# A decoder layer on one core: first and last rows of every engine's queue written as sequences of their own, weights prepared step by step between them

## The reference

```python
# attention: 8 heads of 128; x is (32, 112, 256), wq, wk, wv (256, 8, 128), wo (8, 128, 256)
q, k, v = einsum(layernorm(x), wq), einsum(.., wk), einsum(.., wv)
q, k = rope(rmsnorm(q)), rope(rmsnorm(k))
p = softmax(q k^T / 128 with a causal mask)
x = x + (p v) wo
# the context (32, 375, 256) serves as both weights of a two-layer net
h = layernorm(x) @ ctx^T
x = x + gelu_tanh(h) @ ctx
# a quantised feed-forward net (FFN): 256 -> 1024 -> 256
xq = fixed_quant(layernorm(x), 8, 4); w1q, w2q, b1q, b2q = fixed_quant(.., 8, 6)
x = x + fixed_quant(relu(fixed_quant(xq @ w1q^T + b1q)), 8, 4) @ w2q^T + b2q
```

## Time and profile before

| | |
|---|---|
| median of 3 runs | 654.29 us (653.25 to 656.85) |
| the profiled execution | 654.7 us, its span 652.9 us |
| PE, matmuls | 593.3 us busy, 91% |
| DVE | 588.1 us busy, 90% |
| ACT | 543.0 us busy, 83% |
| POOL | 348.0 us busy, 53% |
| mean granted PE clock | 0.974 |

### The profile page before, as it was taken

How to read it: one execution, slowest core, us unless ns; L and a number is a source line. 1 busy time by engine, 2 the same in 40 slices (tenths; PEclk the granted TensorE clock), 3 DMA queues, 4 the chain that set the end, 5 groups by cost and what they waited for, 6 DMA issues and landing times.

```text
span 652.9 us, 13103 instructions
## 1 busy us (share of the span) xinstructions
PE 593.3 (91%) x4624; PEld 477.3 (73%) x4624; DVE 588.1 (90%) x1339; ACT 543.0 (83%) x1402; POOL 348.0 (53%) x430
## 2 busy tenths in 40 slices
PE   1746889999999999999999999999999999997864
PEld 1424667777887788888778877888887788776753
DVE  3768899999999999999999999999999999998442
ACT  6675788999999999989998899999889999998522
POOL 1134555665555565666655555656666555556111
PEclk9967999999999999999999999999999999999978
DMA  8071566766776766667687676666677777666451
GB/s 296 0 200 36 114 139 138 137 138 150 149 148 137 147 133 142 141 141 153 133 151 152 143 152 138 137 142 132 143 149 138 150 152 146 134 141 138 89 109 37
DMA packets 222641, 88.92 MB, mean 136 GB/s; under 512 B 200704, under 2 KB 217552, under 8 KB 222320
## 3 DMA queue, kind: packets, MB, share of 16 engines
q1 hardware_dynamic: 222576, 88.08, 63.6%
HBM read 34.84 MB, written 3.67 MB: 59 GB/s over the span
## 4 chain that ended last, share of the span: by engine, by line
DVE 75%; ACT 9%; PE 5%; POOL 3%; issue 3%; DMA 3%; SPq 0%; ACTq 0%; DVEq 0%
DVE turn_s L433 11%; DVE turn_c L425 8%; DVE qk L524 8%; DVE o L550 5%; DVE ss L566 5%; DVE turn_c L614 5%; DVE ss L603 5%; DVE qk L639 4%; DVE h_t L590 2%; DVE y_out L545 2%; DVE g L628 2%; DVE x L634 2%; DVE stat L534 1%; POOL turn_c L354 1%; DVE xn L600 1%
## 5 line engine op out<-in xcount | busy, mean ns | idle before, releaser
L912 PE MATMUL psum<-wqkv,xT 128*112 128x512 f16 x384 | 148.3, 386 | 12.5 <-DMA xT<-xn 9.1
L913 PE MATMUL psum<-wqkv,xT 128*112 128x512 f16 x384 | 147.4, 384 | 0.0
L914 PE MATMUL psum<-wqkv,xT 128*112 128x512 f16 x384 | 147.1, 383 | 0.0
L354 POOL TENSOR_TENSOR turn_c<-turn_c,turn_s 112x1024 f32<-112x1024 f32 x32 | 75.7, 2365 | 48.4 <-DVE turn_s L433 48.4
L912 PEld LDWEIGHTS psum<-wqkv,xT 128*112 128x112 f16 x384 | 50.7, 132 | 43.4 <-DMA xT<-xn 9.7
L425 DVE TENSOR_TENSOR turn_c<-psum,cos_t 112x1024 f32<-112x1024 f32 x64 | 77.8, 1215 | 0.0
L433 DVE TENSOR_TENSOR turn_s<-psum,sin_t 112x1024 f32<-112x1024 f32 x64 | 77.7, 1214 | 0.0
L914 PEld LDWEIGHTS psum<-wqkv,xT 128*112 128x112 f16 x384 | 50.7, 132 | 34.1 <-issue 1.9
L922 PE MATMUL psum<-wo,oT 128*112 128x256 f16 x256 | 71.0, 277 | 4.7 <-DMA oT<-o 3.5
L524 DVE SCALAR_TENSOR_TENSOR qk<-turn_c,rms,qk 112x128 f16<-112x128 f32 x256 | 69.2, 343 | 2.6 <-ACT qk L796 2.5
L924 PE MATMUL psum<-wo,oT 128*112 128x256 f16 x256 | 71.0, 277 | 0.0
(11 more groups left out here) (107 smaller groups left out, 1699.2 us busy)
## 6 DMA issues: line engine op xcount, KB each, us to landing
ctxT<-in_ctx_cols SPq DMA_DIRECT2D x32, 375.0 KB, 3.4
ctx_in<-in_ctx_rows SPq DMA_DIRECT2D x32, 375.0 KB
x_in<-in_x SPq DMA_DIRECT2D x32, 112.0 KB, 2.3
out_y<-y_out SPq DMA_DIRECT2D x32, 112.0 KB, 2.9
w_raw<-in_w SPq DMA_DIRECT2D x2, 1024.0 KB, 6.1
w_raw<-in_wk SPq DMA_DIRECT2D x2, 512.0 KB, 5.0
...
```

What stands on the lines that cost most here:

```text
L354: pool.tensor_tensor(turn_c[:, 1, :], turn_c[:, 1, :], turn_s[:, 1, :], ALU.add).then_inc(k_turned, 1)
L912: pe.matmul(dst, hi, wqkv[:, 0, c, w, cols], start=c == 0, stop=False)
L913: pe.matmul(dst, hi, wqkv[:, 1, c, w, cols], start=False, stop=False)
L914: last = pe.matmul(dst, lo, wqkv[:, 0, c, w, cols], start=False, stop=c == MC - 1)
```

## The change

The three loops over bodies become, on each of the five engines, start(), the loop `for i in range(5, B - 5): body(i)` with the full bodies in the old order and without the `inside` tests, and end(). start() and end() list the calls of the first and last rows one by one, in an order of their own for each engine. The weight steps are cut into smaller calls and stand in start() among the batches' steps; each weight has semaphores of its own. w2 is now staged in w_raw where wq was and w1 where wk was, each loaded as soon as that weight is split; the weights' sums go to PSUM bank 6 (v0's) instead of 2. Where the new order no longer implies what a step needs, a wait is added for those batches, and others are dropped. No arithmetic is added or left out. The diff, cut to its core:

```diff
-        place = w_raw[:, :, :, :].rearrange("p c w n -> p (c w n)")
-        w1_raw = place[:, 0:2 * HD]
-        w2_raw = place[:, 2 * HD:4 * HD]
+        w1_raw = w_raw[:, :, 1, :]
+        w2_raw = w_raw[:, :, 0, :]
...
-        w_sum_ps = psum[:, 2, 0:4]
+        w_sum_ps = psum[:, 6, 0:4]
...
+            def load_w1():
+                sp.wait_ge(w_lo_done[1], MC)
+                sp.dma_start(w1_raw, w1_cols.rearrange("p (c n) -> p c n", c=MC)).then_inc(w1_in, 16)
+
+            def load_w2():
+                sp.wait_ge(w_lo_done[0], MC)
+                sp.dma_start(w2_raw, w2_cols.rearrange("p (c n) -> p c n", c=MC)).then_inc(w2_in, 16)
...
             def load_ctxT(j):
+                if j.off == 2:
+                    sp.wait_ge(h_ready, done(j.plus(-2)))
...
             def transpose_xq(j):
                 sp.wait_ge(xq_done, done(j))
+                if j.off == B - 4:
+                    sp.wait_ge(f1_ready, done(j.plus(-1)))
+                if j.off == B - 1:
+                    sp.wait_ge(f0_ready, done(j.plus(-1)))
...
             def load_ctx(j):
+                if j.off >= B - 4:
+                    sp.wait_ge(ctxout_ready, done(j.plus(-2)))
...
                 sp.wait_ge(xn_lo_done, done(j))
                 if j.has(1):
                     sp.wait_ge(v1_ready, done(j.plus(-1)))
+                if 2 <= j.off <= 4 or j.off == B - 1:
+                    sp.wait_ge(v0_ready, done(j.plus(-1)))
                 sp.dma_start_transpose(xT16[:, :, :], xn16[:, :, :].rearrange("t l n -> t (l n)")).then_inc(xT_landed, 16)
...
+            def start():
+                load_projection(1, 0)
+                load_projection(0, 1)
+                load_projection(1, 1)
+                load_projection(0, 0)
+                load_x(Batch(0))
+                load_projection(2, 0)
+                load_projection(2, 1)
+                load_x(Batch(1))
+                load_x(Batch(2))
+                load_tables()
+                load_ctxT(Batch(0))
+                load_ident()
+                transpose_x(Batch(0))
+                load_x(Batch(3))
+                load_wo()
+                load_ctxT(Batch(1))
+                load_w2()
+                transpose_x(Batch(1))
+                transpose_q(Batch(0))
+                transpose_k(Batch(0))
+                transpose_x(Batch(2))
+                transpose_q(Batch(1))
+                transpose_k(Batch(1))
+                transpose_o(Batch(0))
+                load_ctx(Batch(0))
+                load_biases()
+                transpose_x(Batch(3))
+                load_x(Batch(4))
+                transpose_k(Batch(2))
+                transpose_q(Batch(2))
+                transpose_o(Batch(1))
+                load_ctxT(Batch(2))
+                transpose_x(Batch(4))
...
+                transpose_k(Batch(B - 1))
+                transpose_q(Batch(B - 1))
+                store_out(Batch(B - 7))
+                transpose_o(Batch(B - 2))
+                load_ctxT(Batch(B - 2))
+                load_ctx(Batch(B - 2))
+                transpose_xq(Batch(B - 4))
+                load_ctxT(Batch(B - 1))
+                store_out(Batch(B - 6))
+                transpose_o(Batch(B - 1))
+                load_ctx(Batch(B - 1))
+                store_out(Batch(B - 5))
+                transpose_xq(Batch(B - 3))
+                store_out(Batch(B - 4))
+                transpose_xq(Batch(B - 2))
+                transpose_xq(Batch(B - 1))
+                store_out(Batch(B - 3))
+                store_out(Batch(B - 2))
+                store_out(Batch(B - 1))
+
+            start()
...
@@ vector
+            def start():
+                bound_weights(1)
+                stats_x(Batch(0))
+                lift_weights(1)
+                normalise_x(Batch(0))
+                stats_x(Batch(1))
+                bound_weights(0)
+                split_xn(Batch(0))
+                split_projection(1, 0)
+                lift_weights(0)
+                split_projection(1, 1)
+                normalise_x(Batch(1))
+                stats_x(Batch(2))
+                bound_weights(2)
+                split_projection(0, 0)
+                lift_weights(2)
+                split_xn(Batch(1))
+                split_projection(0, 1)
+                split_projection(2, 0)
+                sum_squares_k(Batch(0))
+                turn_sin_k(Batch(0))
+                turn_cos_k(Batch(0))
+                split_projection(2, 1)
+                bound_weights(3)
+                sum_squares_q(Batch(0))
+                turn_cos_q(Batch(0))
+                turn_sin_q(Batch(0))
+                turn_q(Batch(0))
+                normalise_x(Batch(2))
+                stats_x(Batch(3))
+                split_q(Batch(0))
+                split_k(Batch(0))
+                sum_squares_k(Batch(1))
+                turn_cos_k(Batch(1))
+                turn_sin_k(Batch(1))
+                sum_squares_q(Batch(1))
+                turn_sin_q(Batch(1))
+                split_xn(Batch(2))
+                turn_cos_q(Batch(1))
+                turn_q(Batch(1))
+                normalise_x(Batch(3))
+                split_q(Batch(1))
+                lift_weights(3)
+                invert_sums(Batch(0))
+                split_k(Batch(1))
+                turn_sin_k(Batch(2))
+                sum_squares_k(Batch(2))
+                split_o(Batch(0))
+                turn_cos_k(Batch(2))
+                unit_of_y()
+                split_wo()
+                turn_sin_q(Batch(2))
+                sum_squares_q(Batch(2))
+                turn_cos_q(Batch(2))
+                split_xn(Batch(3))
...
+                split_k(Batch(B - 1))
+                split_q(Batch(B - 1))
+                residual_attention(Batch(B - 3))
+                stats_x2(Batch(B - 3))
+                clip_hidden1(Batch(B - 6))
+                gelu_inner(Batch(B - 4))
+                split_o(Batch(B - 2))
+                gelu_outer(Batch(B - 4))
+                residual_out(Batch(B - 6))
+                normalise_x2(Batch(B - 3))
+                residual_ctx(Batch(B - 4))
+                stats_x3(Batch(B - 4))
+                clip_hidden0(Batch(B - 5))
+                gelu_inner(Batch(B - 3))
+                quantise_x3(Batch(B - 4))
+                clip_x3(Batch(B - 4))
+                invert_sums(Batch(B - 1))
+                residual_attention(Batch(B - 2))
+                split_o(Batch(B - 1))
+                gelu_outer(Batch(B - 3))
+                clip_hidden1(Batch(B - 5))
+                stats_x2(Batch(B - 2))
+                residual_out(Batch(B - 5))
+                normalise_x2(Batch(B - 2))
+                residual_ctx(Batch(B - 3))
+                stats_x3(Batch(B - 3))
...
@@ scalar
+            def start():
+                square_projection(1, 0)
+                square_projection(1, 1)
+                square_projection(0, 0)
+                square_projection(0, 1)
+                round_projection(1, 0)
+                round_xn(Batch(0))
+                square_projection(2, 0)
+                round_projection(1, 1)
+                square_projection(2, 1)
+                round_projection(0, 0)
+                round_projection(0, 1)
+                round_xn(Batch(1))
+                round_projection(2, 0)
+                square_k(Batch(0))
+                round_projection(2, 1)
+                square_wo(0)
+                square_wo(1)
+                square_q(Batch(0))
+                scale_k1(Batch(0))
+                scale_k0(Batch(0))
+                copy_v0(Batch(0))
+                copy_v1(Batch(0))
+                round_q1(Batch(0))
+                round_q0(Batch(0))
+                round_xn(Batch(2))
+                round_k0(Batch(0))
+                square_k(Batch(1))
+                round_weights(1)
+                square_q(Batch(1))
+                scale_k0(Batch(1))
+                scale_k1(Batch(1))
+                softmax_exp(Batch(0))
+                round_q1(Batch(1))
+                round_q0(Batch(1))
+                round_k0(Batch(1))
+                square_k(Batch(2))
+                normalise_o1(Batch(0))
+                normalise_o0(Batch(0))
+                round_o(Batch(0))
+                copy_v1(Batch(1))
...
+                softmax_exp(Batch(B - 1))
+                relu0(Batch(B - 5))
+                square_h(Batch(B - 3))
+                normalise_o1(Batch(B - 1))
+                normalise_o0(Batch(B - 1))
+                round_o(Batch(B - 1))
+                relu1(Batch(B - 5))
+                tanh_h(Batch(B - 3))
+                relu1(Batch(B - 4))
+                copy_xn2T(Batch(B - 2))
...
@@ tensor
             def project_k(j):
                 pe.wait_ge(xT_landed, landed_once(j))
-                if j.has(3):
+                if 3 <= j.off <= 5 or j.off >= 7:
                     pe.wait_ge(x2_done, done(j.plus(-3)))
+                if j.off == 0:
```

(88 more changed lines are left out.)

1155 lines of the change are left out of this document (847 added, 308 removed).

## The result

Timed in turn with the kernel before on the same chip, 20 runs each, the changed kernel took 656.90 us (653.48 to 659.67) against 654.79 (653.25 to 657.75): a ratio of 1.0033 [1.0017, 1.0048], so 2.2 us slower where 13 us faster were forecast, and outside the range of 627 to 652. Single runs of one kernel lie up to 6 us apart, the longer ones at a lower granted clock (of the changed kernel, the 11 runs at a mean clock of 0.975 to 0.978 have a median of 658.0, the 7 at 0.982 to 0.988 one of 656.1), so what follows rests on ratios and on the order of events inside a profile, not on one profile's total. The profiled run of the changed kernel is one of 657.78.

What follows compares the result with a forecast made beforehand. Bodies were taken as full on PE and VectorE, leaving at most 61 us of idle time at the ends; 654.7 - 6.0 (start) - 7.0 (end) = 641.7, less 0.4 for the median: 641.3 us, range 627 to 652.

Steps and rivals of the forecast that it cites:

- I take -6.0 for hitches that a walk misses: Start: the walk put its end 7 or more us earlier; -6.0 was taken to allow for hitches.
- The walk up to k(2): Start: new queues followed with old durations; first matmuls of k(0), k(1), k(2) at 17.65, 35.4, 50.2 us.
- the wait for exp_done(0): Start: a new wait said to set batch 2's first k projection at 50.2 us, 10.9 earlier.
- From here DVE is full: Start, k(3) to k(5): VectorE full and carrying put-off work; projections at 71.0, 87.0 and 106.0 us, the last -7.8.
- The walk's mark for VectorE: Start: split_q(3) ends at 91.2 us instead of 99.55; VectorE's gain is -6.0 net of put-off work.
- the mark k(2): Start: first matmul of batch 2's k projection, forecast at 50.2 us instead of 61.06.
- rival D: Whole kernel: no gain, as the first bodies give back what was won before; 654 us, chance 0.06.
- Rival A: Start: gaps of 2.1 to 3.8 us drop PE's clock in batches 0 to 3; 663 us, chance 0.08.
- The GELU of 28 releases ctx_out(28) at 602.7 [...] and scores(31) now stands before ctx_hidden(29): 604.3: End, PE: batch 31's scores start at 604.3 us, 3.1 earlier than before.
- The forecast's 36.1: End: invert_sums(31) at 609.8 us and the span's end at 645.9, 36.1 us between them.
- the new SP waits: End, SyncE: added waits end before the transposes queued behind them are due; priced at nothing.
- The uncertain x(1): Start: x(1) landing late could delay VectorE's split of x(0) and push k(0) up to +1.5 us.

Runs made afterwards that it cites:

- e1: New order for the first rows only, old order at the end; 656.77 us, ratio 1.0028 to the kernel before.
- e10: Changed kernel with POOL's power for q(4) earlier, batch 0's bias addition later, and VectorE's w1 clip moved into a wait; 654.20 us, ratio 1.0005.
- e9: Changed kernel with unused matmuls keeping PE busy ahead of k(1) and k(2), 10 and 16 of them; 655.41 us, ratio 1.0023.
- e3: Changed kernel with three two-operand VectorE passes replaced by one-operand reductions in the first seven and last six batches; 653.79 us, ratio 0.9977.
- e5: Separate test without the layer: POOL sums beside VectorE passes; small sums took 0.92 us alone, 4.87 beside two-SBUF-operand sums.
- e11: Changed kernel with the edits of e7, e8, e9 and e10 together; 651.43 us, ratio 0.9944 to the kernel before.
- e13: New start with the edits of e9 and e10, old order at the end; 650.86 us, ratio 0.9943 to the kernel before.
- e15: Kernel before with unused matmuls keeping PE busy, 38 ahead of k(1) and 32 ahead of scores(0); 654.44 us, ratio 0.9990.
- e7: Changed kernel with batch 28's GELU passes straight behind split_q(31) and its tanh ahead of rounding o(30); 653.97 us, ratio 0.9991.
- e8: Changed kernel with FFN steps of batches 27 and 29 moved ahead of batch 31's late steps on PE, ACT and VectorE; 656.10 us, ratio 1.0021.
- e14: Old start, new order at the end with the edits of e7 and e8; 652.20 us, ratio 0.9960 to the kernel before.

## Why the prediction was wrong

**The start: the step that failed is "I take -6.0 for hitches that a walk misses".** That term priced hitches at 1.8 us; by the timed runs they are 7.8 more (e1), by the profile 5.9 (first body at 131.69, forecast 125.8). The walk up to k(2) was right in every mark, and the wait for exp_done(0) decides k(2) as it said. From there it missed three things. First, it gave every POOL instruction its length of before. These lengths held in the old order, where 3 places were lengthened. In the new one VectorE is packed in places (9.96 us of work in the window 60 to 70), POOL's small results fall beside passes with two SBUF operands and come late: summed over the chain's POOL pieces up to the first body, less the lengths of before, 8.3 us. Second, it did not ask what stands ahead of a small result on POOL's own queue (e10: the first body 1.3 us earlier in the profile, 1.8 by the times). Third, k(2) runs at the lower clock after a wait of 3.87 us (e9: 2.2 us earlier in the profile, 0.7 (+-1.8) by the times). "From here DVE is full" was taken as a bound; in fact VectorE waited, late, for what POOL and PE brought late.

That POOL is held is shown (e3, e5); what the hold costs is not. e3, which takes most of it out of the start, brings the first body forward by only 0.5 us in its profile (1.3 counted from the first bound_weights), and there the wo split on VectorE is held in the place of turn_k; and e11 and e13 keep nearly all of the lengthened pieces (67.16 and 68.41 us of POOL work at the start) and are faster than the kernel before. e9 and e10 on the new start together give 5.6 (+-1.9) of the 7.8 back (e13), in the profile of e11 3.3 of the 5.9. The rest of the start's miss stays open.

**The walk's mark for VectorE.** split_q(3) was to end at 91.2 and ended at 94.22 (99.55 before); its idle time before body(5) was to be 22 and is 27.3 (27.8 before). At the mark k(2) it was 6.2 us below the old kernel's, and 5.8 of these were given back between there and the first body. This is the place of rival D ("the first bodies give back what was won before"), which had a chance of 0.06 and no mechanism; for the start it is what happened.

**Rival A** held in one of its pieces: k(2) runs at the lower rate after 3.87 us of waiting (0.72 in its window), as the Trainium skill ("TensorE: Matmul & The Clock Gate", HAM oscillation) says of bursts with waits between them. The pieces from 60 to 110 that A needed show 1.00 in all five windows, though a wait of 2.54 us stands in front of the first of them. What the clock is worth stays open. In e15 hardly anything came of it. In e9 the profile has 2.2 us at the first body, and the times go with the clock: the two runs at a mean of 0.993 took 651.67 and 652.19 us, the four at 0.980 to 0.982 took 657.67 to 658.78. No run tells whether the clock makes the longer time there or longer waits make the lower clock.

**The end: the step that failed is "The GELU of 28 releases ctx_out(28) at 602.7 [...] and scores(31) now stands before ctx_hidden(29): 604.3".** It started at 611.12, 6.8 late. Of these, 3.7 are split_q(31): 0.5 because the last stretch began later (at 527.0, was 526.5), the rest because VectorE waited more in it (4.3 us of idle before split_q(31), 1.1 before the change), one of the waits of 1.22 for a scaling that a late root from POOL held. The other 3.1 are PE's queue: out_units(26), which the walk does not list there, and ctx_out(28) stand ahead of scores(31), both wait for the GELU of 28 (2.82 us, and then 1.96 and 2.77 us at the lower clock). e7 moves that GELU up and gets 2.8 back. The forecast's 36.1 from invert_sums(31) to the end became 38.5: hidden_units1(28) waits 2.34 us on ACT behind round_o(31), and project_out(31) stands behind it. e8 removes that wait and shows no gain that can be told from nothing. Together e7 and e8 are worth 3.2 (+-1.6) of the 7.6 (e14); some 4 us of the end's miss stay open. The runs do not show whether they lie in VectorE's waits ahead of split_q(31) or in the low clock of the last 30 us (0.83 in the window 620 to 630, was 0.66).

**Right:** the middle at 17.97 a body for 17.94, though the 0.6 us that this makes over 22 bodies stand, in like size, in every profile with the new start (395.15 to 395.54 us, 394.62 to 395.12 with the old one); the FFN weights staged over wk and wq, and the new SP waits, which show on no chain; the last 24.1 us behind residual(31), forecast 23 to 24. The uncertain x(1) landed in time in the profile of the change (0.30 us of waiting, 1.0 to 1.5 in eight of the ten other profiles with the new start), inside the bound given.
